# First FFN by tokens sorted to their two experts, in blocks of 256, instead of all eight experts on every token

## The reference

```
x = x + 0.5 * FFN(layernorm(x))
x = x + ATTN(layernorm(x))
x = x + 0.5 * FFN(layernorm(x))      # same weights as the first FFN
```

```
weights = softmax(x @ router_w + router_b); top 2, divided by their sum
out = sum over the two experts e of weight[e] * (gelu(x @ W1[e] + b1[e]) @ W2[e] + b2[e])
```

## Time and profile before

| | us |
|---|---|
| median of three runs | 2146.27 |
| the profiled execution | 2135.63 |
| its span in the profile | 2133.8 |

### The profile page before, as it was taken

The page is one execution under the profiler, slowest core; times in us unless marked ns, Lnnn a source line. Parts: engine busy times, 40 slices in busy tenths (PEclk is TensorE's granted clock), DMA queues, the critical chain, the costliest instruction groups (busy, mean ns, idle before and its releaser), DMA issues.

```text
span 2133.8 us, 40198 instructions
## 1 busy us (share of the span) xinstructions
PE 2024.4 (95%) x13232; PEld 1578.9 (74%) x13232; DVE 1583.7 (74%) x5212; ACT 1243.3 (58%) x2953; POOL 1037.2 (49%) x1150
## 2 busy tenths in 40 slices
PE   7999999989999999999998998998999899999998
PEld 6888888876766666666666665766667688888887
DVE  6988888988676676677576576675765488888887
ACT  5555555656656657657657557567556555555554
POOL 4444445545536447347247246256254444444444
PEclk9999999999999999999999999999999999999999
DMA  6111111000011011011011011011013111111110
GB/s 235 58 60 41 41 41 41 30 21 18 33 40 41 16 54 32 11 60 36 1 65 31 1 65 31 1 65 31 3 52 121 37 40 36 36 39 40 35 36 31
DMA packets 72326, 91.19 MB, mean 43 GB/s; under 512 B 6432, under 2 KB 66232, under 8 KB 71096
## 3 DMA queue, kind: packets, MB, share of 16 engines
q1 hardware_dynamic: 61368, 69.39, 9.5%
q0 software_dynamic: 8448, 18.95, 3.1%
q10 hardware_dynamic: 2304, 0.28, 0.1%
HBM read 40.23 MB, written 48.37 MB: 42 GB/s over the span
## 4 chain that ended last, share of the span: by engine, by line
PE 56%; DVE 21%; issue 9%; POOL 9%; ACT 4%; DMA 0%; DVEq 0%; POOLq 0%; ACTq 0%
PE bank L530 10%; PE bank L532 9%; PE bank L531 9%; PE bank L749 5%; PE bank L738 5%; PE bank L709 4%; PE bank L720 4%; PE bank L681 3%; DVE st L1043 3%; PE bank L557 3%; DVE xb L1133 2%; POOL hl L1373 2%; POOL tri L1348 2%; DVE wt L1104 2%; ACT prob L967 1%
## 5 line engine op out<-in xcount | busy, mean ns | idle before, releaser
L1421 POOL TENSOR_TENSOR prob<-prob,rden 128x512 f32<-128x512 f32 x320 | 335.6, 1050 | 539.4 <-DVE rden L1273 537.3
L1133 DVE SCALAR_TENSOR_TENSOR xb<-bank,gate,xb 128x256 f32<-128x256 f32 x1024 | 423.5, 476 | 91.5 <-PE bank L532 89.9
L1373 POOL TENSOR_TENSOR hl<-hf,hh 128x512 fp32r<-128x512 f32 x256 | 330.2, 1296 | 221.0 <-ACT hh L837 211.9
L967 ACT ACTIVATE prob<-prob,nmax 128x256 f32<-128x256 f32 x512 | 256.2, 503 | 279.9 <-DVE nmax L1255 278.0
L836 ACT ACTIVATE hf<-bank,b1s 128x512 f32<-128x512 f32 x256 | 176.3, 689 | 335.5 <-PE bank L532 328.3
L1255 DVE CUSTOM_DVE_ANT_0 prob<-bank,mask 128x256 f32<-128x256 f32 x512 | 195.2, 418 | 142.8 <-PE bank L709 141.2
L1267 DVE COPY probT<-bank 128x512 f32<-128x512 f32 x160 | 110.3, 689 | 127.2 <-PE bank L720 127.1
L709 PE MATMUL bank<-kT,qT 64*128 64x256 f32 x1024 | 191.6, 429 | 13.7 <-ACT prob L967 9.5
L720 PE MATMUL bank<-ident,prob 128*128 128x128 f32 x1280 | 197.2, 277 | 4.4 <-POOL prob L1421 4.1
L720 PEld LDWEIGHTS bank<-ident,prob 128*128 128x128 f32 x1280 | 156.0, 142 | 58.6 <-issue 17.7
L738 PE MATMUL bank<-probT,V 128*64 128x128 f32 x2048 | 169.1, 286 | 6.2 <-ACT oT_s L983 4.8
(11 more groups left out here) (179 smaller groups left out, 5256.1 us busy)
## 6 DMA issues: line engine op xcount, KB each, us to landing
xb<-in_L_attn_x SPq DMA_DIRECT2D x16, 512.0 KB, 3.8
x_d<-xb SPq DMA_DIRECT2D x16, 512.0 KB, 2.9
x<-x_d SPq DMA_DIRECT2D x8, 1024.0 KB
x_d<-x SPq DMA_DIRECT2D x8, 1024.0 KB, 4.3
xb<-x_d SPq DMA_DIRECT2D x16, 512.0 KB, 3.8
out<-xb SPq DMA_DIRECT2D x16, 512.0 KB, 2.8
hrow<-hs_d SPq DMA_DIRECT2D x16, 257.0 KB, 2.6
w<-w_d SPq DMA_DIRECT2D x4, 1024.0 KB, 11.2
```

The lines of the kernel that those rows point to most:

```text
L967: act.activation(prob[j % NP][:, h, :], src, ACT.Exp, bias=nmax[:, j % 4, h:h + 1], scale=-1.0 if light else 1.0, accum_out=den[:, j % 4, ...
L1133: dve.scalar_tensor_tensor(out=x, in0=bank[ob][:, (t % 2) * D:(t % 2 + 1) * D], scalar=gate[:, k % 2, t, e:e + 1], in1=x, op0=ALU.mult, op ...
L1373: pool.tensor_tensor(lo[:, :], f[:, :], h[:, :].bitcast(F32), ALU.subtract).then_inc(s_hl)
L1421: pool.tensor_tensor(prob[j % NP][:, :, :], prob[j % NP][:, :, :], rden[:, j % 4, :].unsqueeze(2).broadcast_to([P, 2, KEYS]), ALU.mult).th ...
```

## The change

The first FFN is written anew; the second one and the attention stay as they are but for their hooks.

- **Batches.** Rows are taken in batches of 2, 4 and 2 (`BATCH`). For each group: load, statistics, normalize in place (`group_norm`), transpose, logits in one float32 pass, ranks, `chosen` (1 for the two best experts), and by matmuls with a triangle of ones the running number of each token within its expert (`group_spots`). POOL then scatters each tile twice, to the places of its two experts in the DRAM buffer `spots_d` (`send`: 8 indirect DMAs a group, 128 in all).
- **Table.** After the last group of a batch, `batch_table` (16 small DVE operations) works out how many blocks of 256 places each expert needs and in which order, expert and row number of each block; `pads` fills the end of each expert's list with zeros (eight DMAs on SP at addresses read from the table). The blocks of a batch are a fixed number: twice its tokens by 256, plus 7: 23, 39 and 23, 85 in all. Unused ones work on zeros. `batch_homes` works out where each token's two results will stand.
- **Steps.** Each block is one step: SP loads it at an address from a register; PE transposes (4); ACT copies the expert's W1 to a fixed place (`w1_copy`) and writes the high part; DVE the low part; PE computes the hidden layer (6 matmuls of 256 columns); ACT two gelus of 256 columns; POOL their difference; PE the output (6 matmuls of 256 columns) with the expert's W2 at a register's offset; DVE adds b2 of the expert; SP stores the block to `made_d`. PE, ACT, DVE and SP each read a number from SBUF into a register for each step.
- **Ticks.** All of this follows a common clock of ticks (`TICKS`, 114): step s starts at tick 24 + s, and group k at `GROUP_AT[k]`.
- **Combination.** For each row POOL gathers the two results of each tile by 16 indirect DMAs (`fetch`) into y_row and z_row, and DVE adds them to x, read from the input, with their weights (`combine`, 16 operations of 128x256). For row 0 this stands in the ticks of the last batch, for row b > 0 in the slots from 40b - 45 (fetch) and 40b - 39 (combine) on. The statistics that follow go to one tile a slot.
- The lead-in has 20 slots in place of 40; the first two qkv jobs move into the last ticks. The buffer x1_d goes.

The core of the diff:

```diff
+BATCH = ((0, 2), (2, 6), (6, 8))
+BLK = 256
...
+        STEP0 = 24
+        TICKS = STEP0 + STEPS + 5
+        GROUP_AT = (0, 3, 6, 9, 12, 15, 18, 21, 24, 27, 30, 33, 44, 51, 58, 65)
...
+            for tau in range(TICKS):
+                for s_ in step_at(tau - 5):
+                    block_store(s_)
+                for s_ in step_at(tau + 3):
+                    block_load(s_)
...
+            def block_load(s_):
+                n = batch_of(s_)
+                if s_ == FIRST[n]:
+                    pads(n)
+                    sent(sp, n)
+                    sp.wait_ge(s_zero, 16 * E * (n + 1))
+                    sp.wait_ge(s_spare, 16 * (n + 1))
...
+                row = value(sp, block_row[n][0:1, s_ - FIRST[n]:s_ - FIRST[n] + 1], 0, SPARE[n] + (E - 2) * BLK)
+                sp.dma_start(xin[s_ % 4][:, :, :], spots_d[n][bass.ds(row, BLK), :].rearrange("(p s) d -> p s d", s=BT)).then_inc(s_bld[s_ % 4], 16)
...
+            def block_out(s_):
...
+                e = value(pe, block_e[n][0:1, s_ - FIRST[n]:s_ - FIRST[n] + 1], 0, E - 1)
+                w = [x[:, bass.ds(e, 1), :].rearrange("p a n -> p (a n)") for x in w2_s]
...
+                for j in range(BT):
+                    cs = slice(j * P, (j + 1) * P)
+                    ins = mm3(bank[4 + s_ % 2][:, j * D:(j + 1) * D], [hh[s_ % NH][:, cs], hl[s_ % NH][:, cs]], w, start=True, stop=True)
...
+                pool.indirect_dma_start(spots_d[batch_of_group(k)], bass.IndirectOffsetOnAxis(spot[:, k, c, q:q + 1], 0), xb[k % 4][:, q, :], None).then_inc(s_sc[k % 4], 16)
...
+                pool.indirect_dma_start(part[:, t, :], None, made_d[n], bass.IndirectOffsetOnAxis(home[:, 2 * b + t // TG, c, t % TG:t % TG + 1], 0)).then_inc(s_got[i], 16)
...
+                    dve.scalar_tensor_tensor(out=x, in0=part[:, t, :], scalar=share[:, k, c, q:q + 1], in1=x, op0=ALU.mult, op1=ALU.add).then_inc(s_comb)
...
+        def got_slot(b, i):
+            return SLOTS * b - 45 + i // 2
+
+        def add_slot(b, t):
+            return SLOTS * b - 39 + t
...
         def stat1_slot(b, q):
-            return SLOTS * b - 38 + q // 2
+            return SLOTS * b - 38 + q
```

More of the change, by code:

```diff
@@ L165, in build @@
         top[0] = z2
[L166 to L174, removed]
+        ones = sb("ones", [P, P], BF16)
@@ new lines, in build @@
+        sums = sb("sums", [P, TG, E])
+        picks = sb("picks", [P, 2, TG, E])
+        spot_f = sb("spot_f", [P, GROUPS, 2, TG])
+        spot = sb("spot", [P, GROUPS, 2, TG], U32)
+        count = sb("count", [P, E])
+        over = sb("over", [P, E, MAXI])
+        need = sb("need", [P, E])
+        shut = sb("shut", [P, E, E])
+        ahead = sb("ahead", [P, E])
+        until = sb("until", [P, E])
+        base_f = sb("base_f", [P, E + 1])
+        jump = sb("jump", [P, E])
+        passed = sb("passed", [P, MAXB, E])
@@ new lines, in build @@
+        jumps = sb("jumps", [P, MAXB, E])
+        edges = sb("edges", [P, MAXM, E - 1])
+        edge = sb("edge", [P, MAXM])
+        block_f = sb("block_f", [P, 2, MAXB])
+        xa = [sb(f"xa{i}", [P, C, NG]) for i in range(2)]
+        xin = [sb(f"xin{i}", [P, BT, D]) for i in range(4)]
+        w1_s = sb("w1_s", [P, E, 2, C, FF], F32R)
+        w1_now = [sb(f"w1_now{i}", [P, 2, C, FF], F32R) for i in range(2)]
+        w2_s = [sb("w2_hi", [P, E, D], F32R), sb("w2_lo", [P, E, D], F32R)]
+        assert top[0] >= z2 + (HC * N + HC * PADDED + (T + 1) * INNER) * 4
@@ L430, in rank_count, with sent, made @@
                 n += 1
-        CONST = 18
+        CONST = 22
+        NADD = 2
+        def sent(engine, n):
+            for k in range(2 * BATCH[n][1] - 4, 2 * BATCH[n][1]):
+                engine.wait_ge(s_sc[k % 4], 128 * (k // 4 + 1))
+        def made(engine, n):
+            end = FIRST[n] + BLOCKS[n]
+            for i in range(4):
+                engine.wait_ge(s_bst[i], 16 * ((end - 1 - i) // 4 + 1))
         def sp_program():
@@ new lines, in group_spots @@
+            def group_spots(k):
+                pe.wait_ge(s_ra, NA * k + 9)
+                tb = claim(("apos", k, 0))
+                m = chosen[k % 2]
+                pe.matmul(bank[tb][:, 0:(TG + 1) * E], later[:, :], m[:, :, :].rearrange("p t e -> p (t e)"), start=True, stop=False)
+                for d in range(1, TG + 1):
+                    ins = pe.matmul(bank[tb][:, d * E:(TG + 1) * E], ones[:, :], m[:, 0:TG + 1 - d, :].rearrange("p t e -> p (t e)"), start=False, stop=(d == TG))
+                ins.then_inc(s_full)
@@ L897, in evac @@
                 job = (kind, x, i)
-                if kind == "op" and not heavy_tile(x) or kind == "lg":
+                if kind == "op" and not heavy_tile(x) or kind in ("lg", "alg", "apos"):
                     return
@@ L1304, in dve_program @@
+            made(dve, len(BATCH) - 1)
             for u in slots():
```

806 lines of the change are left out of this document (607 added, 199 removed).

## The result

The changed kernel takes 2210.62 us (median of four runs, 2206.16 to 2215.32) against 2147.06 us (2138.19 to 2148.26): a ratio of 1.0306, 95% interval 1.0270 to 1.0341. It is 3.1% slower where 1.4% faster was forecast. The profiled executions are 2209.0 us (span 2207.3) and 2135.6 us (span 2133.8), 73.4 us apart.

A forecast was written before the change was run, and what follows sets the result against it. PE, busy 95% of the span, was taken to bound the kernel. The first exp comes 75 us earlier (414 instead of 489.6), attention pays 45, net 30: 2116 us; range for 8 in 10 2045 to 2215 us.

The forecast's parts named there:

- 6 us for the clock: First stage: PE has gaps in every tick, so the granted clock drops for part of it; 6 us added.
- Then POOL is the longest: First stage, after the first scatter near 25 us: POOL's summed work sets the time, 94 us to tick 24, then 85 us.
- 1.17 us a scatter: POOL's price for one indirect transfer: 1.01 us and 0.16 us between two; eight scatters a group make 9.4 us.
- Both changes of batch: First stage: 17 us from last scatter to step 23 at the first change; the second adds 7 us.
- Ticks 47 to 85: First stage: DVE is the fullest engine, 2.4 us a tick and 0.3 us for registers, 2.7 us a tick, 105 us.
- Rival D: Steps of the first stage: register loads are not hidden, at 2.6 us each; program 2247 us, chance 0.10.
- Rival E: First stage: small pieces halve the DMA rate, blocks come late and 40 us are lost; 2156 us, chance 0.06.
- POOL's crowded slots: Attention: 16 gathers in eight slots where eight scatters stand put POOL 4.8 us over; 3 us a row taken.
- Behind each gather waits the scaling of the probabilities: Attention: PE's transposes wait behind that scaling; 4.5 us of delay are free, so 3 us a row, between 0 and 4.8.
- DVE's sums: Attention: 16 weighted sums a row on DVE, 3.4 us a row: 1.9 us and 1.5 us of contention.
- statistics that go to one a slot: Attention: with the weighted sums they leave DVE 1.9 us more in slots 2 to 5, where 0.1 us is free.
- rival C: Attention pays in full: POOL's 4.8 us and DVE's 12 us a row, seven times, 118 us; 2189 us, chance 0.21.

The follow-up runs named there:

- first experiment: Changed kernel with a group's eight scatters issued in two ticks instead of four and the load into its buffer asked one tick earlier: 2201.3 us, ratio 1.0265.
- second experiment: Changed kernel with the three zero fills of the spare blocks (5.5 MB) moved to ticks 18, 36 and 60: 2209.6 us, ratio 1.0309.
- the sixth: Changed kernel with scatters four a tick for twelve groups, then one; pads issued once the table is there; half of attention's gathers eight slots earlier: 2128.3 us, ratio 0.9946.
- the fifth: Changed kernel with four scatters a tick and loads a tick earlier for the first twelve groups, one scatter a tick for the last four: 2164.8 us, ratio 1.0113.
- thirteenth experiment: The sixth with the kernel before's slots for the next row's statistics, normalizations and transposes, and the sums two a slot: 2138.6 us, ratio 0.9991.
- fourth experiment: Changed kernel with half of the gathers of attention rows 1 to 7 issued eight slots earlier: 2185.4 us, ratio 1.0205.

## Why the prediction was wrong

**The first stage, 414 us forecast and 486.4 measured.** By the terms of the sum (forecast in brackets): to the end of POOL's tick 23 it is 130 us (94); from there to the end of its last scatter of batch 1, in tick 43, 114 (85); to PE's first block of that batch 17 (17); to PE's first block of the next batch, in tick 86, 125 (105 and 7); to the end of the ticks 77 (78); lead-in 23 (22). The 6 us for the clock are within these.

- The step that failed is "Then POOL is the longest", in the first two terms, 65 of the 72 us missed. I added up what POOL does and never asked whether its input would be there. The ring of four buffers was in the program; the trace before even had the load (4 us to landing for 512 KB) and the scatter, from which the 8.4 us loop can be built. Scatters spaced otherwise win 44 us. The rest is about what two more errors give. The start was late (first scatter at 34.97 us, not 25: POOL takes the power of group 1 ahead of it, and with it waits for that group's routing). And a price was wrong: 1.17 us a scatter holds where a tensor operation stands between two; back to back it is 1.27, 0.30 us between them, which makes 13.3 us a group of POOL's own work instead of 12.4 (by estimate 11 us for twelve groups). With the ring's wait out of the way (first experiment) POOL is the bound there, as forecast.
- Both changes of batch were sized about right: 17 us for the first, and PE's wait of 6.0 us for the first block in the second, where 7 were forecast. With the pads early both waits go, 9.4 us.
- Ticks 47 to 85 were forecast at 2.7 us each ("the fullest engine is DVE"). They take 3.05 (118.9 us without PE's wait), 14 us more in all, and the fullest engine is PE, with 99.0 us at a mean clock of 0.91, before DVE with 80.5 (2.06 a tick). No engine is full there either; what sets these ticks was not tried. PE's work in the whole stage, put at 220 us, keeps it busy for 292, part of it at the lower clock. The last 28 ticks (2.8 forecast, 2.75 measured) were right. The window of ticks 47 to 85, in the columns of the earlier trace rows:

```profile
261.15:380.05 118.90, 99.03 (x732) 93.59 (x732) 80.48 (x201) 82.00 (x173) 68.68 (x87) 0.91 0.65 218
```

- Rival D (register loads) is out: eight pads, each with a load, take 6.8 us, 0.85 each against 0.43 for an issue, so at most 0.42 us a load where it is in the way; ticks without a group come down to 1.95 us.
- Rival E is out: 5.5 MB moved elsewhere change nothing (second experiment), and the sixth moves the same bytes in a stage that is 54 us shorter, at 230 GB/s instead of 208.
- The clock: 6 us was too little to show what it does. Length times (1 - clock) is 53 us for the stage, 3.4 before. With the ring's wait gone it is 65 us in the first experiment and 41 in the fifth and the sixth. What it costs there was not tried alone.

**Attention, 45 us forecast and 77 measured.**

- POOL's crowded slots, 3 us a row forecast, measured 3.8. "Behind each gather waits the scaling of the probabilities" was right.
- DVE's sums, 3.4 forecast, measured 3.5. But the reason was only half right: leaving out one of two additions gives all of it, so it is not a price for each of DVE's 16 operations. The sum of length times (1 - clock) falls with it, from 46.1 to 30.7 us; how much of the 3.5 us comes that way was not tried.
- What is missing is the timetable: "statistics that go to one a slot" stands in the text as a load on DVE, and the later y, z and transposes that go with it were priced at nothing. Without gathers and additions they are 2.2 to 3.5 us a row (156.8 against 154.6 and 153.3), the third part of the 10.9; with the additions in, undoing them brings nothing (thirteenth experiment), so this third part holds only in the order in which the parts were taken out.
- Row 1 has its share as well (11.7 us).

The marks for rival C were met (additions of 0.87 us on the mean, a row over 162 us), and its side came true, but not its sum: it had attention at 118 us and a first stage that won 75. Its 0.75 us for an addition is what DVE shows only where POOL collides; apart, it is 0.60. The forecast took rows for durations and its own adding up for the pace; both misses are waits between steps that had a price each.

## What to carry to other kernels

Where buffers form a ring, price the loop (last reader issued, landed, load issued, landed, first use) and put it beside the work that stands between in each in-order queue. The pace is the work ahead of the last reader, and then the longer of the loop and the work behind that reader: here 9.5 us and the longer of 8.4 and 3.5. So how the transfers are spread over the ticks can move the time more than their number. In a queue shared with another stage the same burst costs the other stage its length: give a burst only where nothing else waits there. When a change moves steps to other slots to make room, price the moved steps too, and look at the granted clock beside the time: here the same losses of clock came with rows of different length, so it is a thing to look at and not a price.

## What the runs showed of the hardware

Of the 128 additions of DVE (two SBUF inputs each) 40 take over 1 us in the changed kernel, and 37 of these end 0.28 to 0.30 us after a tensor operation of POOL. DVE's timeline beside POOL's above (990.94 + 1.05 = 991.99):

```profile
990.24 2.04 DVE L1516 SCALAR_TENSOR_TENSOR x<-y_row,share,x 128x256 f32<-128x256 f32 x1
992.38 0.48 DVE L1516 SCALAR_TENSOR_TENSOR x<-z_row,share,x 128x256 f32<-128x256 f32 x1
```

It ends at 992.28. The one at 999.79 us takes 3.05 us, over two scalings in a row that end at 1002.55. The Trainium skill ("SBUF — State Buffer", Who interferes with whom) calls the ports that the two engines share an exclusive lock, which a DVE instruction with two SBUF inputs contends for with a GpSimd instruction that reads SBUF; the trace agrees in that these additions are held to the end of the scaling. It leaves one thing open: the addition at 990.24 begins 0.70 us before the scaling, beside a scatter, and is not done before it, while the one at 992.38, beside a gather, takes its 0.48 us. The first addition of a tile takes 1.14 us on the mean where the slot's order puts it there, and 0.58 in the fourth experiment, where the same addition stands beside fewer transfers.

Two indirect transfers back to back on POOL have 0.30 us between them, one behind a tensor operation 0.16 to 0.20. And a first stage whose instructions are the same (but for one semaphore in the last) ends at 432.7, 441.3 or 444.8 us with different attention behind it; why stays open.
